# A transformer layer with routed experts: second norm's rows moved to ScalarE and GpSimd, last outputs by heads, a fourth key buffer and another first attention step

## The reference

```python
B, T, D, H, P = 4, 512, 512, 16, 128        # batches, tokens, width, heads, head width
mod = (silu(c) @ wmod).reshape(4, 6, 1, -1) # sa, ca, ga, sb, cb, gb
h = layernorm(x) * (1 + ca) + sa
x = x + ga * attention(h, Wq, bq, Wk, bk, Wv, bv, Wo, bo)   # causal, 16 heads
h = layernorm(x) * (1 + cb) + sb            # "the second norm"
x = x + gb * ffn(h)                         # 2 of 8 experts for each token, and 2 shared experts, F = 352
```

## Time and profile before

| | before |
| --- | --- |
| median of 3 runs | 1600.01 us (1599.44 to 1600.08) |
| profiled execution | 1593.91 us |
| its span | 1592.0 us |
| PE, PEld busy | 1524.9 us (96%), 1355.5 us |
| DVE, ACT, POOL busy | 1029.9, 727.7, 677.8 us |
| chain that ended last | PE 80%, DVE 9%, DMA 3%, issue 3%, ACT 2%, POOL 2% |
| the core's mean granted clock | 0.988 |

### The profile page before, as it was taken

The page is one execution under the profiler, slowest core; times in us unless marked ns, Lnnn a source line. Parts: engine busy times, 40 slices in busy tenths (PEclk is TensorE's granted clock), DMA queues, the critical chain, the costliest instruction groups (busy, mean ns, idle before and its releaser), DMA issues.

```text
span 1592.0 us, 29527 instructions
## 1 busy us (share of the span) xinstructions
PE 1524.9 (96%) x8844; PEld 1355.5 (85%) x8844; DVE 1029.9 (65%) x2248; ACT 727.7 (46%) x1728; POOL 677.8 (43%) x721
## 2 busy tenths in 40 slices
PE   6899999996999999999999999987999999999998
PEld 3677778885999999999999999876898899999987
DVE  5876566665777777777777777787757422222268
ACT  3542222254666666666666666641222233333333
POOL 2113333344656566656566656554212311111055
PEclk8999999999999999999999999999999999999999
DMA  7334555567757666666757574657213455665556
GB/s 261 131 122 176 199 202 192 197 232 266 224 173 223 181 209 181 213 198 189 216 171 229 150 240 148 203 175 268 86 40 139 166 192 192 239 243 197 196 186 192
DMA packets 203243, 304.02 MB, mean 191 GB/s; under 512 B 80336, under 2 KB 142160, under 8 KB 196000
## 3 DMA queue, kind: packets, MB, share of 16 engines
q1 hardware_dynamic: 193312, 276.82, 51.4%
q0 software_dynamic: 5680, 18.62, 3.9%
q10 hardware_dynamic: 4176, 7.60, 1.6%
HBM read 187.35 MB, written 115.64 MB: 190 GB/s over the span
## 4 chain that ended last, share of the span: by engine, by line
PE 80%; DVE 9%; DMA 3%; issue 3%; ACT 2%; POOL 2%; POOLq 0%; SPq 0%; ACTq 0%; DVEq 0%
PE bank L1432 45%; PE bank L1527 12%; PE bank L1640 7%; PE bank L1592 7%; PE bank L1623 4%; DMA keys<-k_ring 2%; PE bank L1689 2%; PE bank L1445 1%; PE bank L1725 1%; POOL h L1118 1%; DVE h L2181 1%; DVE h L2184 1%; POOL acc L1110 1%; ACT prob L1262 0%; DVE acc L1966 0%
## 5 line engine op out<-in xcount | busy, mean ns | idle before, releaser
L1432 PE MATMUL bank<-w,xt_hi 128*128 (+2 forms) x1136 | 282.7, 331 | 7.5 <-POOL sign L1090 3.0
L1432 PEld LDWEIGHTS bank<-w,xt_hi 128*128 128x128 f32 x1136 | 198.0, 189 | 14.2 <-issue 8.4
L1432 PE MATMUL bank<-w,xt_lo 128*128 (+2 forms) x568 | 184.5, 325 | 0.0
L1274 ACT ACTIVATE prob<-prob,row_inv 128x128 f32<-128x128 f32 (+3 forms) x256 | 137.2, 560 | 82.0 <-DVE row_inv L2075 81.8
L2202 DVE TENSOR_TENSOR ht_lo<-bank,ht_hi 128x128 fp32r<-128x128 f32 (+1 forms) x213 | 48.4, 281 | 169.0 <-ACT ht_hi L1369 168.9
L1262 ACT ACTIVATE prob<-bank,neg_max 128x128 f32<-128x128 f32 (+3 forms) x256 | 133.6, 525 | 48.6 <-DVE neg_max L2067 48.4
L1432 PE MATMUL bank<-w,ht_hi 128*128 (+3 forms) x426 | 140.5, 411 | 15.3 <-DVE ht_lo L2202 15.2
L1432 PE MATMUL bank<-wv_hi,h_hi 128*128 128x256 f32 x512 | 147.8, 289 | 1.0 <-DVE acc L1975 1.0
L1432 PE MATMUL bank<-wv_hi,h_lo 128*128 128x256 f32 x512 | 145.0, 283 | 0.0
L1432 PE MATMUL bank<-wv_lo,h_hi 128*128 128x256 f32 x512 | 145.0, 283 | 0.0
L910 POOL CAST q_hi<-q_raw 128x512 fp32r<-128x512 f32 x64 | 71.0, 1110 | 136.5 <-PE bank L1592 118.5
(11 more groups left out here) (231 smaller groups left out, 4135.6 us busy)
## 6 DMA issues: line engine op xcount, KB each, us to landing
keys<-k_ring SPq DMA_DIRECT2D x64, 512.0 KB, 3.0
ch_raw<-wexp SPq DMA_DIRECT2D x128, 170.0 KB, 3.1
experts_hi<-ch_hi SPq DMA_DIRECT2D x128, 170.0 KB, 2.6
experts_lo<-ch_lo SPq DMA_DIRECT2D x128, 170.0 KB, 2.7
w<-experts_hi SPq DMA_DIRECT2D x10, 2176.0 KB, 7.9
w<-experts_lo SPq DMA_DIRECT2D x10, 2176.0 KB, 14.5
q_transposed<-q_out SPq DMA_DIRECT2D x64, 256.0 KB, 2.0
k_even<-keys SPq DMA_DIRECT2D x16, 1024.0 KB, 5.7
```

The costliest lines, as they stand in the source:

```text
L1274: ins = act.activation(part, part, ACT.Copy, scale=row_inv[:, h, r:r + 1])
L1432: ins = pe.matmul(dst, a, m, start=(k == 0), stop=(k == last))
```

## The change

It has five parts.

1. **Key ring.** A fourth buffer, used from half 20 of stage 1 on (`ring_slot`).
2. **First attention step.** The scores go to banks 2, 6, 7, 2, 3, 6; the third piece stands before the values of tile 2, the values of tile 3 after the sixth piece; `v_part(0)` stands after most of the softmax. The queries of step 2 are loaded early, to the buffer of the value weights. SyncE loads the keys of step 2, the parts of h and two chunks of expert weights ahead of the last three key stores, and waits for all key stores before it loads the output weights. The bias rows are copied by GpSimd, tile by tile.
3. **Last outputs by heads.** The four output tiles of the last step are made for head 0, then for head 1, ahead of job 0; the turn of row tile 1 stands before job 0; VectorE's `gate_columns` and rows of tiles 2 and 3 of batch 0 stand at the end of the step; the statistics of batch 1 stand between the last adds.
4. **Rows of batches 1 to 3.** ScalarE writes (x - mean) * rstd (one instruction, with -mean*rstd, which GpSimd makes, as bias); GpSimd multiplies by (1 + cb) and adds sb (two instructions).
5. **Loads.** All tiles of the shared jobs come by SyncE's queue; the rows are stored two tiles at a time; the load of x for batch 2 stands after the first tile.

```diff
+def s_bank(i, at_first):
+    return (2, 6, 7, 2, 3, 6)[i] if at_first else 2 + i % 2
+def ring_slot(n):
+    return n % 3 if n < 4 * K_NO[MOD_DONE] else n % 4
...
 # SyncE, end of stage 1
                 if v == NV - 2:
                     load_h(0)
+                    sp.wait_ge(wv_ok, 1)
+                    sp.wait_ge(q_ld, 16)
+                    sp.dma_start(q_early[:, :, :], q_v[:, 1, :, 0:64]).then_inc(q_ld, 16)
+            def first_loads():          # after the first key store of the last half
+                sp.wait_ge(w_full, 7 * NV)
+                load_k(1, 1)
+                sp.wait_ge(h_ld, 32)
+                load_h(1)
+                for s in range(2):
+                    sp.dma_start(ch_raw[:, s, :], wexp[:, s * CH:(s + 1) * CH]).then_inc(ch_ld[s], 16)
...
+            for e in range(4):
+                sp.wait_ge(k_st[e], 16 * ring_uses(e, 4 * NK))
             sp.dma_start(wo_raw[:, :, :], wo_v[:, 0:2, :]).then_inc(wo_ld, 16)
...
 # SyncE, end of the last step
-                    for k in range(2):
-                        store_h2(0, k, k + 1)
-                        sp.wait_ge(h2_st, 16 * (k + 1))
-                        sp.dma_start(xin[:, k, :].unsqueeze(1), rows_t[:, k:k + 1, :]).then_inc(xin_ld[k], 16)
+                    store_h2(0, 0, 1)
+                    sp.wait_ge(h2_st, 16)
+                    load_xin(0)
+                    load_xr(tail)
+                    store_h2(0, 1, 2)
...
                     load_shared(0, WG, WU)
+                    sp.wait_ge(h2_st, 32)
+                    load_xin(1)
...
-            store_h2(1)
+            half_stored(1, 0)
+            sp.wait_ge(h2_st, h2_stored(1) - 16)
+            load_xin(4)
+            load_xin(5)
...
+            half_stored(3, 0)
+            sp.wait_ge(h2_st, h2_stored(3) - 16)
+            load_xin(12)
             sp.wait_ge(wo_add, NIT * TT)
             load_w(E + 1, 1)
-            store_h2(2)
-            store_h2(3)
+            load_xin(13)
+            half_stored(3, 1)
...
 # GpSimd
+            def c_rows(b, t):
+                row, n = h2[:, t, :], (b - 1) * TT + t + 1
+                pool.wait_ge(c_xa, n)
+                pool.tensor_tensor(row, row, mods[:, b, 2, :], ALU.mult).then_inc(c_scaled, 1)
+                pool.wait_ge(c_scaled, n)
+                pool.tensor_tensor(row, row, mods[:, b, 1, :], ALU.add).then_inc(h2_ok, 1)
...
+                if first:
+                    split_q(1)
+                    pool.wait_ge(kh_ok, 4 * NK)
+                    bias_rows(1)
+                    for e in range(4):
+                        pool.wait_ge(k_st[e], 16 * ring_uses(e, 4 * NK))
...
+            c_rows(1, 0)
+            c_rows(1, 1)
+            shared_y(0)
+            c_rows(1, 2)
+            c_rows(1, 3)
+            shared_y(1)
+            loaded(3)
+            c_pre(3, range(0, 2))
+            c_seed_of(2)
+            shared_y(2)
+            c_pre(3, range(2, TT))
+            shared_y(3)
+            c_rows(2, 0)
+            c_rows(2, 1)
...
 # ScalarE
+            def c_rows(b, t):
+                act.wait_ge(c_seed, (b + 1) * C_SEED)
+                act.wait_ge(h2_st, h2_stored(b - 1))
+                act.activation(h2[:, t, :], acc[:, b * TT + t, :], ACT.Identity, scale=rstd[:, t:t + 1],
+                               bias=nt1[:, t:t + 1]).then_inc(c_xa, 1)
+            ROWS_AT = {0: (1, 0), 1: (1, 2), 4: (2, 0), 5: (2, 2), 8: (3, 0), 9: (3, 2)}   # after job n
...
 # TensorE
+            for i in range(3):
+                last_out(i, 0)
+            pe.wait_ge(o_ok, NIT * 2)
+            last_out(3, 0)
+            for i in range(TT):
+                last_out(i, 1)
+            turn_rows(1, 1, loaded(1, 1, False))
             pe.wait_ge(g_ok, 1)
             pe.wait_ge(we_ld[0], 32)
             half(0, 0, 0, 0, True)
-            for i in range(TT):
-                out_tile(NIT - 1, HP - 1, i, None)
```

More of the change, by code:

```diff
@@ L279, in adaln_layer @@
         s1.close()
-        ring = [k_ring[:, e] for e in range(3)]
+        ring = [k_ring[:, e] for e in range(4)]
         mod_row = {0: q_out[0:B, 2, :], 1: q_out[0:B, 3, :], 3: ct[0][0:B, :], 2: mod_a, 4: mod_a, 5: mod_a}
@@ L940, in _, with c_pre @@
             stage1_over(pool)
-            for e in range(3):
-                pool.wait_ge(k_st[e], 16 * len([k for k in range(4 * NK) if k % 3 == e]))
-            def c_pre(b):
-                def scaled(t):
+            def c_pre(b, tiles=range(TT)):
+                for t in tiles:
                     a = acc[:, b * TT + t, :]
@@ L986, in split_q, with bias_rows @@
                 def split_q(h):
-                    split(q_in[:, h], q_nat_hi[:, h], q_nat_lo[:, h],
+                    split((q_in_early if first else q_in)[:, h], q_nat_hi[:, h], q_nat_lo[:, h],
                           [(q_ld, n * 16 + 32), (s_full, n * 6 + (3 * h + 3))], q_ok)
+                def bias_rows(m):
+                    for t in range(m * TT, m * TT + TT):
+                        pool.tensor_copy(acc[:, t, :], bo_b[:, :]).then_inc(acc_ok, 1)
                 def chunk(q):
@@ L1006, in step @@
                     chunk(q)
-                if not last:
+                if not last and not first:
                     split_q(1)
@@ L1325, in step @@
                     xt_part(0, 0)
+                if first:
+                    for e in range(4):
+                        act.wait_ge(k_st[e], 16 * ring_uses(e, 4 * NK))
                 o_part(0)
@@ L1343, in _, with job @@
             walk_steps(act, step)
-            def job(n, s, prev, nxt, tile=None, batch=None, route=False):
+            def job(n, s, prev, nxt, tile=None, route=False):
                 act.wait_ge(gt_full, n + 1)
@@ L1669, in step @@
                 scores(5, n, here)
+                if first:
+                    values(3)
                 turn(0)
@@ L1756, in _ @@
             half(0, 0, 0, 0, True)
-            for i in range(TT):
-                out_tile(NIT - 1, HP - 1, i, None)
             pe.wait_ge(we_ld[1], 32)
             half(0, 0, 0, 1, True)
-            turn_rows(1, 1, loaded(1, 1, False))
             pe.wait_ge(wo_add, NIT * TT)
```

365 lines of the change are left out of this document (201 added, 164 removed).

## The result

The changed kernel takes 1572.4 us (1569.1 to 1574.3, 4 runs) beside 1599.7 us (1599.3 to 1600.1, 4 runs) of the kernel before: ratio 0.9827, 95% interval 0.981 to 0.9844. The forecast was 1575.5, in a range of 1568 to 1589. In two later sets of runs the same pair gave ratios of 0.9844 (0.9816 to 0.9873) and 0.9831 (0.9812 to 0.985). The kernel before stood at 1591 to 1594 us in these, not at 1600, so medians are compared only within a set. By medians the gain is 27.3 us in the first set and 23.7 and 28.4 in the two later ones.

A forecast was written before the change was run, and what follows sets the result against it. TensorE bounds the kernel (80% of the chain), with time to gain only in two seams. Terms 8.6 + 5.6 + 10.2 = 24.4 us, taken from the 1600.0 us median, gave 1575.5 us, range 1568 to 1589.

The forecast's parts named there:

- the middle: Attention from 404 to 1058 us: TensorE busy 651.2 of 654 us at full clock, so nothing to gain.
- D: Rival: more than 31 us gained, VectorE's chain before job 1 ending at 1074 (4.9 more), clock staying high; chance 0.07.
- C: Rival: GpSimd's row instructions bound the shared jobs; slower from 2.3 us each, 1610 us at 2.54; chance 0.11.
- First seam: First attention step, 367 to 404 us: earlier scores, bias copies moved and new order gain 8.6 us.
- The key ring: End of stage 1: a fourth buffer removes ScalarE's key store wait, scores begin at 371.3 instead of 374.6; 3.3 us.
- The order: First attention step: other banks and order let three score pieces run ahead; 1.5 us after allowances for waits and contention.
- The bias rows: First attention step: two copies of 1906 ns leave ScalarE's chain before the probabilities, GpSimd takes them; 3.8 us.
- VectorE beside GpSimd: First attention step: GpSimd's new work holds up VectorE's small instructions; 1.5 us lost, bound 0 to 10.
- Second seam: Between attention and the shared jobs, 1058 to 1156 us: earlier job 1 and later waits removed gain 15.8 us.
- From the last turn to job 1: First row tile's wait goes, VectorE's chain bounds, with 1.8 us contention: job 1 at 1078.6 instead of 1084.2; 5.6 us.
- The jobs behind: Shared jobs behind 1084 us: row writing leaves VectorE, so its hidden low parts are no longer late; 10.2 of 11.8 us.
- B: Rival: the first attention step gives nearly nothing, through slow neg_max beside GpSimd or late output weights; 1584 us, chance 0.20.

The follow-up runs named there:

- e11: The changed kernel with the first attention step's old order and banks and the late load of step 2's queries; 1573.7 us, ratio 0.9887 to the kernel before.
- e9: The changed kernel with the load of x for batch 2 back ahead of the store and first row tile's load on SyncE's queue; 1567.5 us.
- e3: The changed kernel with the rows of batches 1 to 3 written by VectorE again, none by ScalarE and GpSimd; 1574.8 us.
- e10: The changed kernel with job 0's gate product ahead of the last output products again, its up product and row tile 1's turn behind them; 1567.1 us.
- e4: The changed kernel with VectorE writing row tile 1's low part and first hidden product ahead of batch 1's statistics; 1569.0 us.
- e6: The kernel of e4 with ScalarE's rows of batch 1 behind jobs 1 and 2 instead of 0 and 1; 1564.4 us.

## Why the prediction was right, and where it was not

**The time.** 27.3 us were gained beside 24.4 forecast. The sum was made against the profiled execution and carried over to the median; by the traces the gain is 22.1 us, and 28.8 up to the routed jobs. So the total agrees partly by luck: I had no term for the 3.8 us in the middle, where the prediction says that nothing can be gained, nor for the 6.7 at the end, of which the two later traces have 4.3 and -0.8. Two numbers of the rivals were off without changing the sum: job 1 at 1074 instead of 1078.6 would give 4.6 us and not 4.9 (D), and the 2.54 us of C is the row of two additions, 1.27 us each.

**First seam, 8.6 forecast, 9.7 to 11.0 measured, with the wrong terms.** The key ring was 3.3, measured 5.3 to 5.7 when undone alone, of which the later start of the scores is 1.9. The order was 1.5, measured 2.0 to 2.4. The bias rows were 3.8 and are 0 to 0.7. The failing step is "Two bias copies of 1906 ns stand in this chain before and leave it": they stand in ScalarE's list, but behind the last normalising for which TensorE waits 3.30 us, and what follows them has cover. In their place are the queries of step 2. The prediction had their split near 378, where it came, but used that only as room for GpSimd's copies and gave it no term: undone alone they cost 6.5 to 6.9 us. These single prices sum to more than the whole seam, so they overlap; e11 shows it for two of them. What I called late next (queries' split, then scores at 371.3) came at 371.5; the step's last product came at 393.7 instead of 395.0.

**VectorE beside GpSimd.** 1.5 us were set for it in the first step; there `neg_max` on two columns takes 552 ns in the mean of three, 0.3 more than the 231 of before in the same step, so it is about 1 us of VectorE's time. The place where it mattered is the middle stretch, and it is a gain. It comes from a part of the change that its five points leave out, in GpSimd's `c_pre`:

```diff
+                for t in tiles:
...
+                    pool.tensor_tensor(a, a, mods[:, b, 0, :], ALU.mult).then_inc(x1_scaled, 1)
+                    pool.wait_ge(x1_scaled, b * TT + t + 1)
+                    ins = pool.tensor_tensor(a, a, xr[:, t, :], ALU.add)
```

Timeline of POOL in the kernel before, beside the long `neg_max`:

```profile
1013.18 1.28 POOL L949 TENSOR_TENSOR acc<-acc,mods 128x512 f32<-128x512 f32 x1
1014.42 1.29 POOL L959 TENSOR_TENSOR acc<-acc,xr 128x512 f32<-128x512 f32 x1
```

Timeline of POOL in the changed kernel:

```profile
1000.64 1.31 POOL L1015 TENSOR_TENSOR acc<-acc,mods 128x512 f32<-128x512 f32 x1 [2.10 <-issue]
1002.02 1.29 POOL L1017 TENSOR_TENSOR acc<-acc,xr 128x512 f32<-128x512 f32 x1
1003.27 1.29 POOL L1015 TENSOR_TENSOR acc<-acc,mods 128x512 f32<-128x512 f32 x1
1004.64 1.30 POOL L1017 TENSOR_TENSOR acc<-acc,xr 128x512 f32<-128x512 f32 x1
```

and of VectorE beside it:

```profile
1003.48 1.11 DVE L2205 TENSOR_SCALAR neg_max<-row_max 128x2 f32<-128x2 f32 x1
```

The last row answers to the 5.11 us of the earlier trace rows. Before, `c_pre` scaled tile t + 1 ahead of the addition of tile t, and GpSimd's instructions followed each other without a gap; now the addition waits for the scaling of its own tile, and between the two is a gap of 0.07 us (1000.64 + 1.31 to 1002.02; 1003.27 + 1.29 to 1004.64). VectorE's instruction ends at 1004.59, in such a gap. The step there takes TensorE 17.2 us from turn to turn, where before it took 20.8: there it waited 1.02 and 0.49 us and then ran at half clock, which the 1.00 of the whole stretch in the earlier trace rows hides. Busy times of the kernel before, columns as in the earlier trace rows:

```profile
1022.00:1026.00 4.00, 3.99 (x11) 3.13 (x12) 2.40 (x6) 2.65 (x6) 2.29 (x2) 0.57 0.51 199
```

Some of the 3.6 us is lost again in the next step, where VectorE's rows meet `c_pre` (19.4 us against 18.6, and 20.8 in the two later traces). I had read the reordering of `c_pre` as nothing. That the gap is the cause is read from the traces and was not tried alone. For it: no `neg_max` in these two steps is over 1.11 us in any of the three traces of the changed kernel. Against it as the whole rule: another VectorE instruction of the kernel before meets GpSimd where its instructions follow each other without a gap, and is held for one only. Timelines of DVE, then of POOL before:

```profile
1062.40 1.20 DVE L2190 TENSOR_TENSOR w<-g_raw,w 128x32 fp32r<-128x32 f32 x1
```

```profile
1062.29 1.26 POOL L959 TENSOR_TENSOR acc<-acc,xr 128x512 f32<-128x512 f32 x1
1063.51 1.26 POOL L949 TENSOR_TENSOR acc<-acc,mods 128x512 f32<-128x512 f32 x1
```

It ends at 1063.60, right behind the first of them; in the changed kernel it takes 0.19 us in the first trace, where it falls between two of GpSimd's, and 1.23 in the second. So the kind of VectorE's instruction, or the moment at which it comes, may count as well.

The rule of the Trainium skill ("SBUF — State Buffer", § Who interferes with whom), one GpSimd instruction as the price of a meeting, fits the 1.11 us here and not the 5.11. It also fits VectorE's rows in front of job 1, timeline of the changed kernel:

```profile
1044.11 0.74 DVE L2328 SCALAR_TENSOR_TENSOR h<-acc,mean_var,mods 128x512 f32<-128x512 f32 x1
...
1052.61 1.79 DVE L2328 SCALAR_TENSOR_TENSOR h<-acc,mean_var,mods 128x512 f32<-128x512 f32 x1
...
1054.44 1.67 DVE L2331 SCALAR_TENSOR_TENSOR h<-h,rstd,mods 128x512 f32<-128x512 f32 x1
```

One lasts 1.05 us longer beside `c_pre(2)` than alone, less than a GpSimd instruction of 1.3.

**Second seam, 15.8 forecast, 15.1 measured.** From the last turn to job 1 it is 26.0 us before and 20.3 after: 5.6 gained, as forecast (6.2 in the two later traces). The meeting with GpSimd cost 3.0 us in three instructions of the rows (1.05, 0.92 and 1.05), less the 1.0 us that the gate columns lost before and in this trace don't: 2.0, where I had 1.8. The first row tile has no wait, as forecast; e9 shows that SyncE's queue did it. The jobs behind gave 9.5 of 10.2; e3 puts 7 to 8 of it down to the rows, mostly as forecast. e10 shows a piece ahead of job 1 that I had not seen: the output products cover the load of job 0's weights.

**The rivals.** B (first step gives little) and C (GpSimd bounds the jobs) did not come. GpSimd's row instructions take 1.29 us (the multiplication below, and 1.288 the addition), not 1.38, far from the 2.3 at which C decides. Group of the changed kernel:

```profile
L1030 POOL TENSOR_TENSOR h<-h,mods 128x512 f32<-128x512 f32 x12 | 15.5, 1290 | 0.8 <-ACT h L1461 0.8
```

The move of the loads to SyncE's queue cost nothing that this trace shows; in the other traces of the same kernel TensorE waits 0.39 and 0.66 us for one row tile. Whether ScalarE's queue would be better was not tried.

## What to carry to other kernels

An instruction that leaves an engine's list gains only if the engine is waited for behind it: look for the first wait of the bounding engine after its place, not at the engine's busy time (the bias rows). When a stage gets shorter, list the loads that its old length hid; here one of them, the queries, cost more when late (6.5 us) than the key ring that the change was read to remove (5.3). When statistics or rows move on one engine, move their consumers on the next engine too, or its whole queue stands (e4 and e6).
